# A mixture-of-experts kernel: token rows gathered as quarter rows and turned by VectorE instead of TensorE

## The reference

```
x = x + tanh(g_xattn) * softmax(masked((ctx Wq + bq)(ctx Wk + bk)^T / 16 * layernorm(x)))
h = layernorm(x)
probs = softmax(h @ gate_w.T)            # 64 experts, top 8 per token, weights normalised
for each expert e: its first 256 tokens (in token order) are its rows
    out_e = (silu(h_e @ wg[e]) * (h_e @ wu[e])) @ wd[e]      # 1024 -> 384 -> 1024
x = x + tanh(g_ffn) * sum over the token's experts of weight * out_e
```

## Time and profile before

| | us |
|---|---|
| median of 3 runs | 2090.3 |
| the runs | 2084.61, 2091.12, 2090.3 |
| span of the profiled execution, from first to last instruction | 2089.3 |

### The profile page before, as it was taken

One profiled execution on the slowest core, in us unless ns is written; L12 is line 12 of the kernel. 1 busy time (PEld: TensorE's weight loads), 2 busy tenths in 40 slices (PEclk: granted clock), 3 DMA queues, 4 the chain that ended last, 5 costly groups with the idle time before them and its releaser, 6 DMA issues.

```text
span 2089.3 us, 37900 instructions
## 1 busy us (share of the span) xinstructions
PE 1924.5 (92%) x13696; PEld 1429.0 (68%) x13760; DVE 1313.1 (63%) x2221; ACT 1143.8 (55%) x1507; POOL 811.9 (39%) x751
## 2 busy tenths in 40 slices
PE   7777777529999999999999999999999999999998
PEld 3444444427777777777777777777777777777775
DVE  5766666536666666666666666666666666666663
ACT  5555555425555555555555555555555555555553
POOL 0788788762323332333232333322222322332321
PEclk9999997659999999999999999999999999999999
DMA  5465443227888888888888888888888888888883
GB/s 219 150 237 185 134 137 134 94 77 248 272 275 276 279 277 279 276 278 276 264 264 267 270 266 270 275 276 278 278 278 278 278 278 266 264 266 269 267 269 74
DMA packets 90632, 501.27 MB, mean 240 GB/s; under 512 B 17761, under 2 KB 19553, under 8 KB 65505
## 3 DMA queue, kind: packets, MB, share of 16 engines
q1 hardware_dynamic: 45536, 362.24, 43.7%
q0 software_dynamic: 45056, 138.58, 29.9%
HBM read 396.69 MB, written 104.07 MB: 240 GB/s over the span
## 4 chain that ended last, share of the span: by engine, by line
PE 78%; POOL 11%; issue 8%; DMA 1%; POOLq 0%; DVE 0%; ACT 0%; SPq 0%; DVEq 0%
PE ps_gu L454 48%; PE ps_d L463 24%; POOL place_table L923 10%; PE ps_x L439 5%; POOL norm L916 1%; PE ps_j L369 0%; PE ps_s L380 0%; DMA b_qk<-in_bqT 0%; PE ps_t L369 0%; DMA xg<-h_rows,g_idx 0%; POOLq L923 0%; DMA place_table<-token_no,where 0%; POOLq L94 0%; DMA table<-place_table 0%; DVE xb L792 0%
## 5 line engine op out<-in xcount | busy, mean ns | idle before, releaser
L980 POOL DMA_INDIRECT out<-ob,s_idx x128 | 207.2, 1619 | 1051.5 <-ACT ob L632 1029.8
L454 PE MATMUL ps_gu<-xT,split_g 128*128 128x256 bf16 x4608 | 536.2, 273 | 0.0
L454 PE MATMUL ps_gu<-xT,split_u 128*128 128x256 bf16 x4608 | 534.4, 273 | 0.0
L463 PE MATMUL ps_d<-split_d,act 128*128 128x512 bf16 x2240 | 493.9, 379 | 3.4
L454 PEld LDWEIGHTS ps_gu<-xT,split_g 128*128 128x128 bf16 x4608 | 451.9, 98 | 65.1
L454 PEld LDWEIGHTS ps_gu<-xT,split_u 128*128 128x128 bf16 x4608 | 450.9, 98 | 52.2
L838 DVE TENSOR_TENSOR split_d<-raw_d,split_d 128x1536 bf16<-128x1536 f32 x128 | 219.3, 1755 | 398.6 <-ACT split_d L615 398.6
L463 PEld LDWEIGHTS ps_d<-split_d,act 128*128 128x128 bf16 x2304 | 225.4, 98 | 258.2
L923 POOL DMA_INDIRECT place_table<-token_no,where x256 | 294.0, 1148 | 77.6 <-issue 77.3
L619 ACT ACTIVATE sil<-ps_gu 128x256 f32<-128x256 f32 x192 | 73.7, 384 | 445.3 <-PE ps_gu L454 445.3
L632 ACT ACTIVATE ob<-ps_d,wcol 128x512 f32<-128x512 f32 x256 | 171.3, 687 | 259.0 <-PE ps_d L463 259.0
(11 more groups left out here) (86 smaller groups left out, 1426.0 us busy)
## 6 DMA issues: line engine op xcount, KB each, us to landing
raw_g<-in_wg SPq DMA_DIRECT2D x64, 1536.0 KB, 11.6
raw_u<-in_wu SPq DMA_DIRECT2D x64, 1536.0 KB, 15.7
raw_d<-in_wd SPq DMA_DIRECT2D x64, 1536.0 KB
h_rows<-hrow SPq DMA_DIRECT2D x34, 544.0 KB, 3.6
xb<-in_x SPq DMA_DIRECT2D x32, 512.0 KB, 5.0
out<-xb SPq DMA_DIRECT2D x32, 512.0 KB, 2.7
ctx_sb<-in_ctxT SPq DMA_DIRECT2D x4, 1024.0 KB, 8.7
place_table<-token_no,where POOLq DMA_INDIRECT x256
```

Source lines behind the costliest of these rows:

```text
L454: mm = pe.matmul(ps_gu[m][:, t, :], w[:, wi, k, m * P:(m + 1) * P], xT[u][:, k, xi, :], start=(k == 0 and (wi, xi) == (0, 0)), stop=(k == ...
L463: mm = pe.matmul(ps_d[n % 3][:], act[u][:, ai, m, half * P:(half + 1) * P], split_d[:, wi, m, c * NH:(c + 1) * NH], start=(m == 0 and (wi, ...
L980: p.indirect_dma_start(out=out, out_offset=bass.IndirectOffsetOnAxis(ap=s_idx[u][:, half:half + 1].bitcast(U32), axis=0), in_=ob[u][:, hal ...
```

## The change

A token's row is stored as four quarter rows of 256 + 64 floats, with the 64 expert weights behind each quarter; the features are dealt out so that a quarter q holds, of each 128 features, those numbered 32q to 32q + 31. A gather instruction g fetches for 32 token slots all four quarters into 128 partitions (32 slots x 4 quarters), so an expert has eight gather DMAs of 128 pieces of 1280 bytes in place of two DMAs of 128 rows of 4352 bytes. DVE then transposes blocks of 32 x 32 (`turn`, four instructions per expert of 128 x 512 floats each, from `xg` into a new SBUF tile `xt`), which leaves the features on the partitions. The transposes on PE and their PSUM tile `ps_x` are gone; `turned_high` and `turned_low` read `xt` in SBUF, and `ps_d` has four banks in place of three. The copy of the weights column moves from POOL to DVE (four small copies, one per group of 32 partitions). The order of ACT's program is unchanged; DVE's order has the `turn`s and `weights` in it, and one `gate_low` and one `up_low` are placed ahead of the `turned_low`s. The row table is loaded a second time in the layout of the pieces, by four DMAs, and turned into piece numbers by one DVE operation. The router's weights are loaded by eight DMAs in place of one, with the features in the dealt order. The diff, cut to its core:

```diff
+    QS = 4
+    QH = H // QS
+    QW = QH + E
+    NB = QH // 32
+    NG = CAP // 32
...
-    h_rows = nc.dram_tensor("h_rows", [ROWS, HW], F32, kind="Internal").ap()
+    assert QS * 32 == P and NB == KH
+    h_rows = nc.dram_tensor("h_rows", [ROWS * QS, QW], F32, kind="Internal").ap()
+    h_whole = h_rows.rearrange("(t q) c -> t q c", q=QS)
...
-        hrow = [sb(f"hrow{i}", [P, HW], F32, a_mem) for i in range(4)]
+        hrow = [sb(f"hrow{i}", [P, QS, QW], F32, a_mem) for i in range(4)]
...
-        xg = [sb(f"xg{u}", [P, 2, HW], F32) for u in range(2)]
+        xg = [sb(f"xg{u}", [P, NG, QW], F32) for u in range(2)]
+        xt = sb("xt", [P, KH, CAP], F32)
         xT = [sb(f"xT{u}", [P, KH, 2, CAP], BF16) for u in range(2)]
-        g_idx = [sb(f"g_idx{u}", [P, 2], I32) for u in range(2)]
+        g_idx = [sb(f"g_idx{u}", [P, NG], I32) for u in range(2)]
...
-        ps_x = [ps(f"ps_x{i}", [P, 2, CAP], F32, ctx) for i in range(2)]
-        ps_d = [ps(f"ps_d{i}", [P, NH], F32, ctx) for i in range(3)]
+        ps_d = [ps(f"ps_d{i}", [P, NH], F32, ctx) for i in range(4)]
...
-                sp.dma_start(h_rows[g * P:(g + 1) * P, :], hrow[g % 4][:]).then_inc(h_stored[g % 4], 16)
+                sp.dma_start(h_whole[g * P:(g + 1) * P], hrow[g % 4][:]).then_inc(h_stored[g % 4], 16)
...
-            sp.dma_start(gw_sb[:], gwT).then_inc(small_loaded, 16)
+            for k in range(KH):
+                r = slice(k % QS * 32, k % QS * 32 + 32)
+                sp.dma_start(gw_sb[r, k // QS::2], gwT[:, k].rearrange("(q i) e -> i q e", i=32)).then_inc(small_loaded, 16)
...
-            sp.dma_start(table[:].rearrange("p t e -> p (t e)"),
-                         place_table.rearrange("(p k) o -> p (k o)", p=P)).then_inc(table_loaded, 16)
+            for q in range(QS):
+                sp.dma_start(piece_table[q * 32:(q + 1) * 32], place_table.rearrange("(g r e) o -> r g (e o)", r=32, e=E)
+                             ).then_inc(table_loaded, 16)
+            sp.dma_start(table[:], place_table.rearrange("(t p e) o -> p t (e o)", p=P, e=E)).then_inc(table_loaded, 16)
...
-            def turn(e, u, q, first=False):
-                pe.wait_ge(gathered[u], 16 * (e - u) + 32)
-                if not (first and q < 2):
-                    pe.wait_ge(xT_out, 4 * e + q - 1)
-                for kk in range(2):
-                    for half in range(2):
-                        at = (2 * q + kk) * P
-                        mm = pe.transpose(ps_x[q % 2][:, kk, half * P:(half + 1) * P], xg[u][:, half, at:at + P], ident[:])
-                mm.then_inc(xT_done, 1)
...
-                        mm = pe.matmul(ps_d[n % 3][:], act[u][:, ai, m, half * P:(half + 1) * P],
+                        mm = pe.matmul(ps_d[n][:], act[u][:, ai, m, half * P:(half + 1) * P],
...
-                        pe.wait_ge(down_out, 4 * e - 2 * n)
+                        pe.wait_ge(down_out, 4 * e - 3 + n)
...
-                if not first:
-                    pe.wait_ge(down_out, 4 * e - 1)
-                down_part(u, 2, range(MI)).then_inc(down_done, 1)
-                pe.wait_ge(down_out, 4 * e + 1)
-                down_part(u, 3, range(MI)).then_inc(down_done, 1)
-            def expert(e, u, first=False, last=False):
+                for n in range(2, 4):
+                    if not first:
+                        pe.wait_ge(down_out, 4 * e - 3 + n)
+                    down_part(u, n, range(MI)).then_inc(down_done, 1)
...
                     gate_up(e, u, m, first)
-                    if m < 2 and not last:
-                        turn(e + 1, 1 - u, 2 * m)
-                        turn(e + 1, 1 - u, 2 * m + 1)
...
-                s.activation(hrow[g % 4][:, 0:H], xb[g % 4][:], ACT.Identity, bias=nbias[g % 2][:],
+                s.activation(hrow[g % 4][:, :, 0:QH].rearrange("p q (k i) -> p k q i", i=32),
+                             xb[g % 4][:].rearrange("p (k q i) -> p k q i", q=QS, i=32), ACT.Identity, bias=nbias[g % 2][:],
...
             def turned_high(e, u, q):
-                s.wait_ge(xT_done, 4 * e + q + 1)
-                s.activation(xT[u][:, 2 * q:2 * q + 2, 0], ps_x[q % 2][:], ACT.Copy).then_inc(xT_high, 1)
+                s.wait_ge(turned, 4 * e + q + 1)
+                s.activation(xT[u][:, 2 * q:2 * q + 2, 0], xt[:, 2 * q:2 * q + 2], ACT.Copy).then_inc(xT_high, 1)
...
-                v.scalar_tensor_tensor(hrow[g % 4][:, H:HW], ew[u][:], r8[:, 1:2], fits[:], ALU.mult,
-                                       ALU.mult).then_inc(routed, 1)
+                v.scalar_tensor_tensor(hrow[g % 4][:, :, QH:QW], ew[u][:].unsqueeze(1).to_broadcast([P, QS, E]), r8[:, 1:2],
+                                       fits[:].unsqueeze(1).to_broadcast([P, QS, E]), ALU.mult, ALU.mult).then_inc(routed, 1)
...
+            def turn(e, u, q):
+                v.wait_ge(gathered[u], 16 * NG * (e - u) // 2 + 16 * NG)
+                if not (isinstance(e, int) and e == 0):
+                    v.wait_ge(xT_out, 4 * e + q - 3)
+                v.transpose(xt[:, 2 * q:2 * q + 2].rearrange("p b (g r) -> p b g r", r=32),
+                            xg[u][:, :, 64 * q:64 * q + 64].rearrange("p g (b i) -> p b g i", i=32)).then_inc(turned, 1)
+            def weights(e, u, first=False):
+                if not first:
+                    v.wait_ge(down_out, 4 * e - 4)
+                for q in range(QS):
+                    r = slice(q * 32, (q + 1) * 32)
+                    v.tensor_copy(wcol[u][r], xg[u][r, q::QS, bass.ds(e + QH, 1)].rearrange("p t e -> p (t e)")
+                                  ).then_inc(wcol_ready, 1)
             def turned_low(e, u, q):
                 v.wait_ge(xT_high, 4 * e + q + 1)
-                v.tensor_tensor(xT[u][:, 2 * q:2 * q + 2, 1], ps_x[q % 2][:], xT[u][:, 2 * q:2 * q + 2, 0], ALU.subtract
+                v.tensor_tensor(xT[u][:, 2 * q:2 * q + 2, 1], xt[:, 2 * q:2 * q + 2], xT[u][:, 2 * q:2 * q + 2, 0], ALU.subtract
                                 ).then_inc(xT_out, 1)
             def expert(e, u, first=False, last=False):
@@ -857,23 +868,36 @@
                 down_low(e, 1)
                 activate(e, u, 0, first)
                 if not last:
+                    turn(e + 1, 1 - u, 0)
+                    turn(e + 1, 1 - u, 1)
+                    gate_low(e + 1, 1 - u, 0)
                     turned_low(e + 1, 1 - u, 0)
                     turned_low(e + 1, 1 - u, 1)
-                    gate_low(e + 1, 1 - u, 0)
                     gate_low(e + 1, 1 - u, 1)
                 activate(e, u, 1, first)
                 if not last:
+                    turn(e + 1, 1 - u, 2)
+                    turn(e + 1, 1 - u, 3)
+                    weights(e + 1, 1 - u, first and u == 0)
+                    up_low(e + 1, 1 - u, 0)
                     turned_low(e + 1, 1 - u, 2)
                     turned_low(e + 1, 1 - u, 3)
-                    up_low(e + 1, 1 - u, 0)
                 activate(e, u, 2, first)
...
+            v.wait_ge(table_loaded, 16 * (QS + 1))
+            v.tensor_scalar(piece_table[:].rearrange("p g e -> p (g e)"), piece_table[:].rearrange("p g e -> p (g e)"),
+                            float(QS), piece_no[:], ALU.mult, ALU.add).then_inc(pieces_made, 1)
             for part in range(2):
                 gate_low(0, 0, part)
             for part in range(2):
                 up_low(0, 0, part)
+            for q in range(4):
+                turn(0, 0, q)
+            weights(0, 0, True)
...
             def gather(e, u):
-                chain.link(p.tensor_copy(g_idx[u][:], table[:, :, bass.ds(e, 1)].rearrange("p t e -> p (t e)")))
+                chain.link(p.tensor_copy(g_idx[u][:], piece_table[:, :, bass.ds(e, 1)].rearrange("p g e -> p (g e)")))
                 hold()
-                for half in range(2):
+                for g in range(NG):
                     p.indirect_dma_start(
-                        out=xg[u][:, half, :], out_offset=None, in_=h_rows,
-                        in_offset=bass.IndirectOffsetOnAxis(ap=g_idx[u][:, half:half + 1].bitcast(U32), axis=0),
-                        bounds_check=last_row, oob_is_err=True,
+                        out=xg[u][:, g, :], out_offset=None, in_=h_rows,
+                        in_offset=bass.IndirectOffsetOnAxis(ap=g_idx[u][:, g:g + 1].bitcast(U32), axis=0),
+                        bounds_check=last_piece, oob_is_err=True,
                     ).then_inc(gathered[u], 16)
...
-            def weights(e, u, first=False):
-                p.wait_ge(gathered[u], 16 * (e - u) + 32)
+            def rows(e, u, first=False):
                 if not first:
-                    p.wait_ge(down_out, 4 * e - 4)
                     p.wait_ge(scattered, 32 * e - 32)
-                p.tensor_copy(wcol[u][:], xg[u][:, :, bass.ds(e + H, 1)].rearrange("p t e -> p (t e)")
-                              ).then_inc(wcol_ready, 1)
-                chain.link(p.tensor_copy(s_idx[u][:], g_idx[u][:]))
```

(74 more changed lines are left out.)

1 line of the change is left out of this document (removed).

## The result

The changed kernel takes 2456.35 us (median of four runs, 2455.4 to 2459.01) against 2090.56 before: ratio 1.1753, 95% interval 1.1734 to 1.1771. It is 17.5% slower. The forecast was 2498 us, 1.7% above what was measured, in the range 2350 to 2645.

What follows compares the result with a forecast made beforehand. PE, 92% busy, bounds the kernel before; after, serial DVE and ACT work plus clock loss make a 31.5 us period. 2089.3 + 394 (63 periods) + 12 (start) + 2 (attention) = 2497.3, forecast 2498 us, range 2350 to 2645.

Steps and rivals of the forecast that it cites:

- What bounds it, and what is late next: Experts: PE bounds the kernel before at 25.24 us each; after, `activate` 2 comes late through serial DVE, ACT, DVE work.
- The walk: One expert's DVE and ACT steps from the previous `down`'s end: `activate` 2 ends at 24.02, period 29.20 us before clock loss.
- PE's wait: In `down`, PE runs out of work at 18.34 us and waits 5.7 us for `activate` 2 in every expert.
- The transposes: DVE's four added transposes of 128 x 512 floats per expert: 0.65 us each, 2.6 us together.
- rival 3: DVE's transposes cost 1.22 us each, 2.3 us more per expert on the same path: 2642 us; chance 12%.
- The lower bound of 0.43 us: Lowest price of one DVE transpose of 512, from a cast of 256 at 322 ns.
- The clock: In `down`'s last part of every expert, the low level behind PE's wait costs 1.7 to 3.4 us, 2.3 taken.
- Rival 1: The clock holds through PE's wait, leaving a period of 29.20 us: 2354 us; chance 8%.
- POOL and DMA at nothing: In the expert period, gathers, POOL's issue beside DVE and DMA traffic stay under 31.5 us and cost nothing.
- Start: Before expert 0, table DMAs, more gather issues and POOL held up: +12 us (8 to 18); attention +2.
- Rival 2: In the experts PE stays the bound, 25.24 - 1.75 us each: 1994 us, faster than before; chance 3%.
- The signs: Profile after: PE's share well under 80%, DVE waits for ACT twice, about 2 us each, clock 0.50 in every `down`.

Runs made afterwards that it cites:

- turn_twice: Changed kernel with each of DVE's transposes made a second time into a spare tile; 2668.78 us.
- keep_clock: Changed kernel with 16 extra matmuls of 512 columns into a spare PSUM bank, in down's wait for `activate` 2; 2347.64 us.
- two_gathers: Changed kernel with two of the eight gather DMAs per expert from expert 2 on, computing on partly old rows; 2458.0 us.
- act2_early: Changed kernel with both `split_g` and `split_u` high parts ahead of ACT's `turned_high`s, and DVE's `activate` 2 ahead of `up_low` 0 and `turned_low` 2, 3; 2003.86 us.
- both_first: Changed kernel with ACT's high parts of `split_g` ahead of `turned_high` 0 and 1, and of `split_u` ahead of `turned_high` 2 and 3; 2118.15 us.
- act2_only: Changed kernel with only DVE's `activate` 2 moved directly behind `turn` 3 and the weights, ACT's order unchanged; 2180.68 us.
- gate_first: Changed kernel with one swap in ACT's order: the two high parts of `split_g` ahead of `turned_high` 0 and 1; 2344.49 us.

## Why the prediction was right, point by point

- **What bounds it, and what is late next.** Right. The walk gave the end of `activate` 2 at 24.02 us behind the end of `down`; the trace has it at 1029.09 - 1005.62 = 23.47. The walk's single steps, against the trace: first `turn` at 6.99 (7.00), `gate_low` 0 at 10.46 (10.37), `activate` 1's end at 16.33 (16.12), `up_low` 0 at 19.79 (19.40). A DVE instruction that follows another begins a few hundredths earlier than taken (two of L852 with 1.28 us are 0.60 from start to start, not 0.65), and each of the two hand-offs is 0.1 to 0.2 us shorter; together that makes the 0.55 us.
- **PE's wait.** The sum was 0.6 us too long and its split wrong: 5.7 us at one place were forecast, 0.53 and 4.53 came. The walk itself had `activate` 1 ending at 16.33, behind the 15.77 at which `down` would begin, and the prediction didn't use it. The first 12 matmuls begin late, which costs nothing on the path but shortens the wait behind them.
- **The transposes.** 0.65 us was taken, 686 ns is the mean of all 256, and two take 1.30. turn_twice shows them on the path. The estimate from the Trainium skill's "VectorE: DVE Perf Modes" (The three transpose paths), 1.24 us, is not borne out: the measurement decides, and rival 3 falls. The page gives its figure for bf16; these are float32. The lower bound of 0.43 us was misread: (322 - 159) / 256 is 0.64 ns an element and makes 0.49 us for 512. Nothing rests on it.
- **The clock.** Right in kind, 2.3 us taken. The 24 matmuls take 7.17 us as a mean of 62 periods (6.96 to 7.56) against 5.35 undisturbed (5.15 had been taken), a loss of 1.82; keep_clock gives back 1.75. Rival 1 (2354 us) was the time without this, and keep_clock comes to 2348.
- **The sizes together.** Period 31.5 forecast, 30.71 measured: 0.55 us of it in the walk, 0.28 in the last 24 matmuls (5.15 + 2.3 taken, 7.17 measured). 62 x 0.79 = 49 us too many there, 4.7 too few for expert 0, 1.4 too many for attention and start, 2.4 too few at the end: 43 us, the whole miss of the span (2497.3 forecast, 2454.4 measured). The two mis-sized terms are the walk on DVE and the clock.
- **POOL and DMA at nothing.** Right, shown by two_gathers. The rows that spoke against it are real: a gather DMA takes 1.01 us alone and up to 2.57 beside DVE. The timeline of POOL after, which answers to the earlier trace rows:

```profile
1015.25 1.01 POOL L984 DMA_INDIRECT xg<-h_rows,g_idx  x1 [0.30 <-issue]
1016.57 2.07 POOL L984 DMA_INDIRECT xg<-h_rows,g_idx  x1 [0.30 <-issue]
1018.94 2.56 POOL L984 DMA_INDIRECT xg<-h_rows,g_idx  x1 [0.30 <-issue]
```

  The last two stand beside `gate_low` 0, the `turned_low`s and `gate_low` 1, all with two SBUF inputs. By the rule of the Trainium skill's "SBUF — State Buffer" (Who interferes with whom), a GpSimd read stands still through such an operation; the trace agrees with 2.56 against 1.01. It did not matter because POOL's issue was done at 1024.1, 9 us ahead of its next scatter.
- **Start.** +12 and +2 forecast, +12.6 came. The last scatter of attention starts at 449.84 us instead of 447.88, 2.0 us later, which is luck rather than a reading: act2_early, with the same program in attention, has it at 451.80. What was missed is expert 0: its `turn`s for expert 1 wait 6.06 us for the second gather, which POOL issues only behind the first eight; +11.0 us where 6.3 was in the sum.
- **Rival 2** (PE stays the bound, 1994 us) was the mechanism of the good version: it needed another order, not cheaper transposes.
- **The signs.** DVE, ACT and the clock showed as foretold, the second wait of DVE with 1.45 us for about 2. PE's share did not fall well under 80%: it is 80%, and the walk's own numbers, (23.49 + 2.3) / 31.5, had made it 82%. `turn` 0 waits for the gather only before expert 0 and in expert 0.

## What to carry to other kernels

When work moves from an engine that feeds two others to one of these two, look at the order of both, not at their busy shares: DVE was 63% busy before and 61% after, and the kernel lost 366 us, of which two swaps on the other engine gave back 338. A producer's results that a third engine waits for go ahead of everything that is only needed in the next round. And price a wait on TensorE with what its clock does behind it: here 1.8 of the 5.5 us by which the period grew were the clock, not the wait.

## What the runs showed of the hardware

Between the waits of 1.93 and of 3.03 us lies the step from a wait that costs only itself to one that costs the clock as well; in their regular periods the runs have no wait between them. The last 24 matmuls of `down`, as means over all periods of a run: 5.35 us behind waits of 1.08, 1.63 and 1.93 us (keep_clock, both_first, act2_only), without an exception; 7.55 behind 3.03 us (gate_first), 7.17 behind 4.50 (the kernel after), 8.18 behind 5.71 (turn_twice). In gate_first, whose waits hardly differ, single periods take from 5.35 (two of 63) to 8.32 us, most of them some 7.0 or 8.3. As a mean that wait costs more clock than the one of 4.50. The windows of gate_first show why it can: the clock is whole to the end of the wait and falls when PE already works.

```profile
1022.00:1023.00 1.00, 0.00 (x0) 0.00 (x0) 0.93 (x4) 0.00 (x0) 0.00 (x0) 1.00 0.91 359
1023.00:1027.00 4.00, 3.98 (x11) 1.53 (x12) 1.63 (x1) 1.37 (x2) 0.00 (x0) 0.57 0.18 64
1027.00:1029.00 2.00, 2.00 (x11) 0.88 (x9) 0.00 (x0) 0.69 (x1) 1.63 (x1) 1.00 0.00 0
```

In the expert of the kernel after shown above, 2.4 of some 6.8 us at the lower level pass while PE waits anyway, and only 4.4 us cost.
